# A transformer block on one core: features on partitions to the output, 512-token products, halves added and subtracted, parity checks as matrix products

## The chip, the cores and the metric

The kernel runs on one core of a Trainium2 chip. The metric is device time in microseconds (us) of one execution. The engines are TensorE (PE, with weight loads as PEld), VectorE (DVE), ScalarE (ACT), GpSimd (POOL) and SyncE (SP), which here only issues DMAs.

## The reference

8192 tokens of 256 features; everything is float32.

```python
xn = layernorm(x)                              # over the 256 features, eps 1e-5
D  = fractal_dimension(xn)                     # one number, from the first 1024 values of xn
x1 = ifft(fft(xn) * wave_filter(D)).real       # a circulant 256x256 matrix applied to each token
lat  = x1 @ W_el + b_el                        # 24 latents
bits = sigmoid(lat) > 0.5
syn  = bits @ H.T > 0.5                        # 12 checks; H is 12x24 of zeros and ones
w    = syn.sum(-1)
# if 0 < w <= 3: flip the bits among the first 12 whose check is set; else leave them
attn = x1 + corrected @ W_le + b_le
ffn  = gelu(xn @ w1 + b1) @ w2 + b2            # 256 -> 1024 -> 256, exact gelu
out  = x + attn + ffn
```

## The kernel before

The tokens are cut into 16 chunks of 512 (`CHUNKS`, 4 tiles of 128 tokens each). A float32 operand of a product is split into a part rounded to fp32r (`_hi`) and the rest (`_lo`); each product is the sum of three, hi x hi, lo x hi and hi x lo.

- **up** (L741): w1 is stationary, the normalised input `xT` (features on partitions, 2 blocks `k` of 128) is moving: for each of 8 hidden blocks `m`, 6 products of 512 columns into one of two PSUM banks `p_h`. ACT makes `h` (gelu, L378) and rounds it to `h_hi` (L386), DVE makes `h_lo` (`hidden_lo`, L508).
- **down** (L771): the hidden tile is stationary and w2 moving, so the output has tokens on partitions: for each `m` and each of the 4 tiles 3 products of 256 columns into `p_o`. It waits for the whole of `h_lo`.
- **wave_products** (L790): filter and latents together, 280 columns (256 + 24), 6 for each tile of 128 tokens, into `p_c`, a pair of tiles at a time.
- **correct** (L519, DVE): the bits of a pair of tiles, with tokens on partitions, are weighed with powers of two and summed to a word, and-ed with 12 masks, counted, compared; ten small instructions, most with a wait for the one before (`hops`). PE transposes the result (L805), ACT copies it (L388), and `le_products` (L814) adds it with W_le and both biases (256 columns a tile).
- **The input** comes in twice: rows `x_sb` (kept for all chunks, for statistics and as the residual to which DVE adds in place, L511 and L552) and columns `xt_sb`. Mean and 1/std of each token are made on DVE and POOL, written to DRAM, read back broadcast to all partitions (`rows_sb`, with the four values of a kind 32 bytes apart), and POOL subtracts (L333), DVE multiplies (L498), ACT rounds (L370), DVE takes the rest (L503).

Each engine has its own order of work, written out by hand. Chunk 0 is the prologue: DVE normalises it from rows, PE transposes it, weights are split (`w1_hi`, `w1_lo`, ...), D is found, and the filter's matrix and latent weights are made (`circulant` L868, `latent_products` L875). A loop of 14 chunks follows, each with the branch (filter, bits, correction) of the chunk before, and a last chunk with two branches. PE's order in a chunk is: up m, then pieces of the branch at some m, then down m-2 (L823). DVE's order is at L562, SP's at L294 to L309.

Of the kernel before, what the change touches and what calls it, by code (L numbers as in the profile page):

```python
# [11 lines left out]
P = 128  # L39
# [7 lines left out]
PAIRS = CT // 2  # L47
CE = E + LAT
# [11 lines left out]
HALF = CT // 2  # L60
HEAD = 1
LAST_PIECES = ((0, 2), (2, 3), (3, 4))
PRIMED = 1
ROWS_LE = LAT + 2
# [10 lines left out]
K_POW2 = K_WK + 2 * KB  # L75
K_END = K_POW2 + LAT


def build(nc, x, xt, w_el, b_el, w_le, b_le, w1, b1, w2, b2, consts, prefixes, basis, masks, out):
    ctx = ExitStack()  # L80
    with ctx:
# [20 lines left out]
        w1_f = sb("w1_f", [P, KB, HID], F32)  # L102
        w1_hi = sb("w1_hi", [P, KB, HID], F32R)
        w1_lo = sb("w1_lo", [P, KB, HID], F32R)
        w2_f = sb("w2_f", [P, MB, E], F32)
        w2_hi = sb("w2_hi", [P, MB, E], F32R)
        w2_lo = sb("w2_lo", [P, MB, E], F32R)
        b1_sb = sb("b1_sb", [P, MB], F32)
        con = sb("con", [P, K_END], F32)
        mask_sb = sb("mask_sb", [P, SYN], I32)  # L110
        bel_sb = sb("bel_sb", [P, LAT], F32)
        wel_sb = sb("wel_sb", [P, KB, LAT], F32)
        basis_sb = sb("basis_sb", [P, KB, E], F32)
# [14 lines left out]
        fr_tab = sb("fr_tab", [NS, 3, FR * E], F32)  # L128
        fr_part = sb("fr_part", [NS, FR * E], F32)
# [20 lines left out]
        le_mid = sb("le_mid", [ROWS_LE, E], BF16)  # L150
# [834 lines left out]
```

## Time and profile before

| | us |
|---|---|
| median of 3 runs (445.8 to 446.93) | 446.28 |
| the profiled execution | 446.24 |
| its span | 444.2 |
| PE busy | 433.6 (98%) |
| DVE busy | 298.0 (67%) |
| ACT busy | 197.5 (44%) |
| POOL busy | 80.0 (18%) |

The span goes from the first to the last instruction of the execution. PE's busy time is the union of overlapping matmul records, each of which holds its pipeline's drain, so the price of a product is read from the distance between two starts. A query of the trace prints the start, the duration, the engine, the line, the tiles (written, then read), the shape and how many alike were merged; in brackets the idle time before and what ended it.

### The profile page before, as it was taken

Reading aid. Unit: us, or ns where it says so; the run is one execution under the profiler, and the core shown is the slowest. Engines: PE = TensorE matmul, PEld = TensorE weight load, DVE = VectorE, ACT = ScalarE, POOL = GpSimd, SP = SyncE. Lnnn points to the kernel's source line nnn. Section 1 sums busy time; section 2 is a strip of 40 time slices with the busy share of each in tenths; the row PEclk is TensorE's granted clock in tenths of the full one; section 3 lists DMA queues with packets and bytes.
Section 4 is the critical chain, followed back from the end, with each engine's and each line's share of the span. In section 5 each row is a group of like instructions: output and inputs, shape, how many; then the busy total and the mean of one; then the engine's idle time right before and its main releaser. Section 6 shows DMA issues by size and latency. Waiting matters only on the chain.

```text
span 444.2 us, 8446 instructions
## 1 busy us (share of the span) xinstructions
PE 433.6 (98%) x2856; PEld 391.5 (88%) x2856; DVE 298.0 (67%) x722; ACT 197.5 (44%) x332; POOL 80.0 (18%) x72
## 2 busy tenths in 40 slices
PE   7969999999999999999999999999999999999996
PEld 4858899899999999898998989989999999989996
DVE  5977586665767666576765667666575767667544
ACT  4742444444354344535443444444435434443431
POOL 1640211203013130301213012130401313030000
PEclk9997999999999999999999999999999999999999
DMA  8541302223130232303213230232313022020101
GB/s 236 169 168 48 120 2 90 101 71 118 50 110 29 71 118 71 118 15 99 76 71 118 71 116 2 82 108 71 118 45 106 38 71 71 24 71 5 44 24 49
DMA packets 17789, 35.38 MB, mean 80 GB/s; under 512 B 5331, under 2 KB 7533, under 8 KB 17773
## 3 DMA queue, kind: packets, MB, share of 16 engines
q1 hardware_dynamic: 17778, 35.24, 23.9%
q8 instruction: 6, 0.10, 0.1%
q14 instruction: 5, 0.04, 0.0%
HBM read 26.76 MB, written 8.45 MB: 79 GB/s over the span
## 4 chain that ended last, share of the span: by engine, by line
PE 91%; DMA 3%; POOL 2%; DVE 1%; ACT 1%; issue 1%; SPq 0%; DVEq 0%; POOLq 0%
PE p_o L786 40%; PE p_h L766 38%; PE p_c L800 11%; PE p_c L819 2%; DMA w_f<-L_ffn_w 1%; DMA rows_sb<-rows_dram 1%; PE p_g L810 1%; POOL xt_sb L333 1%; DMA rows_dram<-mv 1%; POOL w_lo L342 1%; PE p_c L872 0%; POOL mv L324 0%; DVE xt_sb L498 0%; DVE x_sb L602 0%; ACT w_hi L419 0%
## 5 line engine op out<-in xcount | busy, mean ns | idle before, releaser
L378 ACT ACTIVATE h<-p_h,b_sb 128x512 f32<-128x512 f32 x128 | 88.1, 689 | 213.0 <-PE p_h L766 213.0
L786 PE MATMUL p_o<-w_hi,h_hi 128*128 128x256 f32 x512 | 149.7, 292 | 4.1 <-DVE h_lo L508 4.1
L786 PE MATMUL p_o<-w_lo,h_hi 128*128 128x256 f32 x512 | 145.4, 284 | 0.0
L786 PE MATMUL p_o<-w_hi,h_lo 128*128 128x256 f32 x512 | 145.2, 284 | 0.0
L508 DVE TENSOR_TENSOR h_lo<-h,h_hi 128x512 fp32r<-128x512 f32 x128 | 94.6, 740 | 52.3 <-ACT h_hi L386 50.0
L786 PEld LDWEIGHTS p_o<-w_hi,h_hi 128*128 128x128 f32 x512 | 98.1, 192 | 7.1 <-DVE h_lo L508 4.7
L786 PEld LDWEIGHTS p_o<-w_lo,h_hi 128*128 128x128 f32 x512 | 98.3, 192 | 1.9
L786 PEld LDWEIGHTS p_o<-w_hi,h_lo 128*128 128x128 f32 x512 | 98.2, 192 | 0.0
L766 PE MATMUL p_h<-xT_hi,w_hi 128*128 128x512 f32 (+1 forms) x258 | 82.1, 399 | 0.6 <-ACT xT_hi L433 0.6
L386 ACT CAST h_hi<-h 128x512 fp32r<-128x512 f32 x128 | 79.5, 621 | 5.6
L766 PE MATMUL p_h<-xT_hi,w_lo 128*128 128x512 f32 (+1 forms) x258 | 79.9, 391 | 0.0
L766 PE MATMUL p_h<-xT_lo,w_hi 128*128 128x512 f32 (+1 forms) x258 | 79.5, 389 | 0.0
L333 POOL TENSOR_TENSOR xt_sb<-xt_sb,rows_sb 128x512 f32<-128x512 f32 x30 | 53.8, 1814 | 83.9 <-DMA rows_sb<-rows_dram 83.9
L498 DVE TENSOR_TENSOR xt_sb<-xt_sb,rows_sb 128x512 f32<-128x512 f32 x30 | 54.0, 1838 | 20.5 <-POOL xt_sb L333 20.5
L766 PEld LDWEIGHTS p_h<-xT_hi,w_lo 128*128 128x128 f32 x258 | 48.3, 188 | 11.1
L766 PEld LDWEIGHTS p_h<-xT_lo,w_hi 128*128 128x128 f32 x258 | 48.3, 188 | 11.0
L321 POOL TENSOR_TENSOR var_eps<-mv,eps 128x4 f32<-128x4 f32 (+1 forms) x17 | 3.8, 225 | 228.3 <-DVE mv L483 228.3
L766 PEld LDWEIGHTS p_h<-xT_hi,w_hi 128*128 128x128 f32 x258 | 41.0, 190 | 2.1 <-ACT w_hi L419 0.8
L560 DVE TENSOR_TENSOR x_sb<-p_c,x_sb 128x512 f32 (+1 forms) x32 | 22.1, 690 | 27.3 <-PE p_c L819 27.3
L800 PE MATMUL p_c<-c_hi,xT_hi 128*128 128x280 f32 x128 | 37.4, 292 | 0.0
L800 PE MATMUL p_c<-c_lo,xT_hi 128*128 128x280 f32 x128 | 37.4, 292 | 0.0
L800 PE MATMUL p_c<-c_hi,xT_lo 128*128 128x280 f32 x128 | 36.9, 289 | 0.0
(95 smaller groups left out, 323.3 us busy)
## 6 DMA issues: line engine op xcount, KB each, us to landing
out<-x_sb SPq DMA_DIRECT2D x31, 256.0 KB, 2.3
x_sb<-L_attn_x SPq DMA_DIRECT2D x15, 512.0 KB, 5.3
xt_sb<-xt SPq DMA_DIRECT2D x15, 512.0 KB, 3.6
rows_sb<-rows_dram SPq DMA_DIRECT2D x15, 512.0 KB, 4.1
w_f<-L_ffn_w SPq DMA_DIRECT2D x3, 512.0 KB, 7.1
x_sb<-L_attn_x SPq DMA_DIRECT2D x2, 256.0 KB, 2.8
w_f<-L_ffn_w SPq DMA_DIRECT2D x2, 256.0 KB, 5.2
basis_sb<-basis SPq DMA_DIRECT2D x1, 256.0 KB, 4.9
```

Source lines behind the costliest of these rows:

```text
L333: nc.gpsimd.tensor_tensor(seg, seg, row_values(par, 0), ALU.subtract).then_inc(centred, 1)
L342: nc.gpsimd.tensor_tensor(w1_lo[:, :, cols], w1_f[:, :, cols], w1_hi[:, :, cols].bitcast(F32), ALU.subtract).then_inc(w1_ready, 1)
L378: nc.scalar.activation(h[m % 2][:], p_h[:, m % 2, :], ACT.Gelu, bias=b1_sb[:, m:m + 1]).then_inc(gelu_done, 1)
L386: nc.scalar.copy(h_hi[m % HR][:], h[m % 2][:]).then_inc(h_hi_done, 1)
L498: nc.vector.tensor_tensor(seg, seg, row_values(par, 1), ALU.mult).then_inc(scaled, 1)
L508: nc.vector.tensor_tensor(h_lo[m % HR][:], h[m % 2][:], h_hi[m % HR][:].bitcast(F32), ALU.subtract).then_inc(h_lo_done, 1)
L560: nc.vector.tensor_tensor(seg, p_c[:, :, 0:E], seg, ALU.add).then_inc(wave_added if last else pair_out, 1)
L766: last = mm(p_h[:, m % 2, tok], w[:, k, m * P:(m + 1) * P], xt[par][:, k, tok], start=(n == 0), stop=(n == 3 * KB - 1))
L786: last = mm(p_o[:, j, :], hp[r][:, tok], w[:, m, :], start=(m == 0 and n == 0 and j % 2 == 0), stop=(m == MB - 1 and n == 2), skip_group_c ...
L800: last = mm(p_c[:, r, 0:CE], xt[par][:, k, tok], cc[:, k, :], start=(n == 0), stop=False, skip_group_check=True)
L810: last = nc.tensor.transpose(p_g[0:3 * SEG, r * P:(r + 1) * P], cor[:, r, :, :].rearrange("p a s -> p (a s)"), id_bf[:])
L819: last = mm(p_c[:, r, 0:E], cor_T[:, r * P:(r + 1) * P], le3[:], start=False, stop=True, skip_group_check=True)
```

## The change

Output, too, has features on partitions from now on, and the host's arrangement of `xt` and `out` follows (moves only).

- The two halves of the features are added and subtracted: `uv` holds x0+x1 and x0-x1 (POOL, `turn`), and w1, w2, the latent weights and W_le are added and subtracted in the same way and halved, once in the prologue (POOL and DVE add, ACT halves and rounds). The filter matrix has the blocks [[A, B], [B, A]], so in this basis it is two 128x128 blocks, A+B and A-B. At the end DVE adds sum and difference to the two halves of the input columns with the bias, four operations of 128x512 in place of the additions before (`add_differences`, `add_sums`).
- **down** has w2 stationary and the hidden block moving: for each `m` 6 products of 512 columns, and it waits for `h_hi` first, for `h_lo` before the last two. The filter adds into the same banks (`p_o`, now two pairs of banks, one for each parity of the chunk).
- **latents**: 6 products of 512 columns for a chunk; the 24 latents stand three times on 96 rows. The bits come out with latents on partitions: `take_bits` is one DVE operation on 96x512, `count` a product with H, `take_checks` a comparison, `weigh` a product with ones, `correct` two operations, `le_products` two products of 512 columns. The word, the masks, the transposes and ACT's copy go.
- The columns `xt_sb` of all chunks stay in SBUF (the last four chunks' places first hold the weights' sums and differences); the rows `x_sb` have two buffers and serve the statistics alone. `rows_sb` is contiguous for each kind of value, and holds twice the mean.
- PE's prologue runs four up blocks ahead of down (`LOOK`). Chunk 1 runs its branch two blocks later than the others (`at`). In the last chunk the two branches, `last_down` with one signal for each half, and four stores.

```diff
-PAIRS = CT // 2
-CE = E + LAT
+HF = E // 2
...
+        xt_sb = sb("xt_sb", [P, CHUNKS, KB, CTOK], F32)
+        x_sb = [sb(f"x_sb{i}", [P, CT, E], F32) for i in range(2)]
+        rows_sb = [sb(f"rows_sb{i}", [P, 2, CTOK], F32) for i in range(2)]
+        uv = sb("uv", [P, KB, CTOK], F32)
...
+        p_o = ps("p_o", [P, 2, 2, BANK], F32)
+        p_l = ps("p_l", [P, BANK], F32)
+        p_g = ps("p_g", [P, BANK], F32)
...
+            def load_x(c):
+                par = c % 2
+                if c >= 2:
+                    sp.wait_ge(stat_done, c)
...
+            def turn_w1(n):
+                cols = slice(W1_PARTS[n][0] * P, W1_PARTS[n][1] * P)
+                pool.wait_ge(w1_in[n], 16)
+                for k, op in ((0, ALU.add), (1, ALU.subtract)):
+                    nc.gpsimd.tensor_tensor(w1_t[:, k, cols], w1_f[:, 0, cols], w1_f[:, 1, cols],
+                                            op).then_inc(w1_turned[n], 1)
...
+            def turn(c, par, first=False):
+                pool.wait_ge(xt_in[par], all_to(c, par))
+                if first:
+                    pool.wait_ge(t_done, 2)
+                else:
+                    pool.wait_ge(t_lo, KB * c)
+                halves = xt_sb[:, bass.ds(c, 1), :, :].rearrange("p c k t -> p (c k) t")
+                nc.gpsimd.tensor_tensor(uv[:, 0, :], halves[:, 0, :], halves[:, 1, :], ALU.add).then_inc(turned, 1)
+                nc.gpsimd.tensor_tensor(uv[:, 1, :], halves[:, 0, :], halves[:, 1, :], ALU.subtract).then_inc(turned, 1)
...
+            def take_bits(c):
+                dve.wait_ge(lat_done, c + 1)
+                nc.vector.tensor_scalar(bits[:], p_l[0:ROWS, :], -1.0, bel_sb[:, 0:1],
+                                        ALU.mult, ALU.is_lt).then_inc(bits_done, 1)
+            def take_checks(c):
+                dve.wait_ge(counted, c + 1)
+                nc.vector.tensor_scalar(syn[:], p_g[0:ROWS, :], 0.5, None, ALU.is_gt).then_inc(syn_done, 1)
+            def correct(c):
+                dve.wait_ge(weighed, c + 1)
+                nc.vector.scalar_tensor_tensor(out=flips[:], in0=p_g[0:ROWS, :], scalar=3.0, in1=syn[:],
+                                               op0=ALU.is_le, op1=ALU.mult).then_inc(flips_done, 1)
+                dve.wait_ge(flips_done, c + 1)
+                nc.vector.tensor_tensor(cor[:], bits[:], flips[:], ALU.not_equal).then_inc(cor_done, 1)
...
+            def add_differences(c, par, tok=slice(0, CTOK), added=diff_added):
+                xc = columns(c, tok)
+                nc.vector.scalar_tensor_tensor(out=xc[:, 0, :], in0=p_o[:, par, 1, tok], scalar=bias[:, 0:1],
+                                               in1=xc[:, 0, :], op0=ALU.add, op1=ALU.add).then_inc(added, 1)
+                nc.vector.scalar_tensor_tensor(out=xc[:, 1, :], in0=p_o[:, par, 1, tok], scalar=-1.0,
+                                               in1=xc[:, 1, :], op0=ALU.mult, op1=ALU.add).then_inc(added, 1)
+            def add_sums(c, par, tok=slice(0, CTOK), done=summed):
+                xc = columns(c, tok)
+                nc.vector.tensor_tensor(xc[:, 0, :], p_o[:, par, 0, tok], xc[:, 0, :], ALU.add).then_inc(done, 1)
+                nc.vector.scalar_tensor_tensor(out=xc[:, 1, :], in0=p_o[:, par, 0, tok], scalar=bias[:, 1:2],
+                                               in1=xc[:, 1, :], op0=ALU.add, op1=ALU.add).then_inc(done, 1)
...
             def chunk(c, par):
+                b = c - 1
+                statistics(c + 1, 1 - par)
+                dve.wait_ge(stats_made, c + HEAD + 2)
                 hidden_lo(c, 0)
-                hops(statistics(c + 1, 1 - par))
+                aggregate(1 - par)
+                take_bits(b)
                 hidden_lo(c, 1)
-                aggregate(1 - par)
-                correct(c - 1, 0, hops)
+                take_checks(b)
                 hidden_lo(c, 2)
+                correct(b)
                 hidden_lo(c, 3)
-                add_wave(c - 1, 0)
+                centre(c + 1, 1 - par)
+                scale(c + 1, 1 - par)
                 hidden_lo(c, 4)
-                scale(c + 1, 1 - par)
+                dve.wait_ge(le_done, c)
+                add_differences(b, 1 - par)
                 hidden_lo(c, 5)
-                correct(c - 1, 1, hops)
+                dve.wait_ge(diff_added, KB * c)
+                add_sums(b, 1 - par)
+                turned_lo(c + 1, 1 - par, 0)
                 hidden_lo(c, 6)
-                transposed_lo(c + 1, 1 - par, 0)
-                transposed_lo(c + 1, 1 - par, 1)
+                turned_lo(c + 1, 1 - par, 1)
                 hidden_lo(c, 7)
-                add_wave(c - 1, 1)
...
+            def last_chunk(c, par):
+                b = c - 1
+                hidden_lo(c, 0)
+                take_bits(b)
+                hidden_lo(c, 1)
+                take_checks(b)
+                hidden_lo(c, 2)
+                correct(b)
+                hidden_lo(c, 3)
+                hidden_lo(c, 4)
+                dve.wait_ge(le_done, c)
+                add_differences(b, 1 - par)
+                hidden_lo(c, 5)
+                take_bits(c)
+                dve.wait_ge(diff_added, KB * c)
+                add_sums(b, 1 - par)
+                hidden_lo(c, 6)
+                take_checks(c)
+                hidden_lo(c, 7)
+                correct(c)
+                dve.wait_ge(tail_down, 1)
...
+            def down(c, par, m, first=False):
+                pe.wait_ge(h_hi_done, MB * c + m + 1)
+                if m == 0 and not (isinstance(c, int) and c < 2):
+                    pe.wait_ge(summed, KB * (c - 1))
                 for n, (m0, _) in enumerate(W2_PARTS):
                     if first and m == m0:
                         pe.wait_ge(w2_ready, n + 1)
                 r = m % HR
...
+                for a in range(2):
+                    for w in (w2_hi, w2_lo):
+                        mm(p_o[:, par, a, :], w[:, m, a, :], h_hi[r][:], start=(m == 0 and w is w2_hi), stop=False,
+                           skip_group_check=True)
+                pe.wait_ge(h_lo_done, MB * c + m + 1)
+                for a in range(2):
+                    last = mm(p_o[:, par, a, :], w2_hi[:, m, a, :], h_lo[r][:], start=False, stop=False,
+                              skip_group_check=True)
+                last.then_inc(down_done, 1)
+            def last_down(c, par, m):
+                pe.wait_ge(h_lo_done, MB * c + m + 1)
+                r = m % HR
+                for a in (1, 0):
+                    for n, (w, hp) in enumerate(((w2_hi, h_hi), (w2_lo, h_hi), (w2_hi, h_lo))):
+                        last = mm(p_o[:, par, a, :], w[:, m, a, :], hp[r][:], start=False, stop=(n == 2),
+                                  skip_group_check=True)
+                    last.then_inc(tail_down, 1)
...
+            def latents(c, par, first=False):
+                if not first:
+                    pe.wait_ge(bits_done, c)
+                n = 0
+                for k in range(2):
+                    for w, xp in ((cw_hi, xT_hi), (cw_lo, xT_hi), (cw_hi, xT_lo)):
+                        last = mm(p_l[0:ROWS, :], w[:, k, :, :].rearrange("p g l -> p (g l)"), xp[par][:, k, :],
+                                  start=(n == 0), stop=(n == 5))
+                        n += 1
+                last.then_inc(lat_done, 1)
...
+            def filtered(c, par):
+                for k in range(2):
+                    for w, xp in ((c_hi, xT_hi), (c_lo, xT_hi), (c_hi, xT_lo)):
+                        last = mm(p_o[:, par, k, :], w[:, k, :], xp[par][:, k, :], start=False, stop=False,
+                                  skip_group_check=True)
...
+            def count(c, first=False):
+                pe.wait_ge(bits_done, c + 1)
+                if not first:
+                    pe.wait_ge(flips_done, c)
+                mm(p_g[0:ROWS, :], code[0:LAT, 0:ROWS], bits[0:LAT, :], start=True, stop=True).then_inc(counted, 1)
+            def weigh(c):
+                pe.wait_ge(syn_done, c + 1)
+                mm(p_g[0:ROWS, :], code[0:SYN, ROWS:2 * ROWS], syn[0:SYN, :], start=True, stop=True).then_inc(weighed, 1)
+            def le_products(c, par):
+                pe.wait_ge(cor_done, c + 1)
+                for a in range(2):
+                    last = mm(p_o[:, par, a, :], le3[:, a, :], cor[:], start=False, stop=False, skip_group_check=True)
...
+                at = (2, 3, 4, 5, 6) if first_branch else (0, 1, 2, 3, 5)
                 for m in range(MB):
                     up(c, par, m)
...
+                    if m == at[0]:
+                        if first_branch:
+                            pe.wait_ge(c_ready, 1)
...
+                    if m == 7:
+                        filtered(c, par)
+                        count(c)
+                down(c, par, MB - 2)
+                weigh(c)
+                le_products(c, par)
+                last_down(c, par, MB - 1)
...
+            for m in range(LOOK):
+                up(0, 0, m, first=True)
             for m in range(MB):
...
+                down(0, 0, m, first=True)
+                if m + LOOK < MB:
+                    up(0, 0, m + LOOK, first=True)
+                if m == 3:
+                    pe.wait_ge(logged, 1)
+                    mm(p_g[:, 0:1], con[0:NS, K_COEF:K_COEF + P], fr_ln[:], start=True, stop=True).then_inc(dim_made, 1)
                 if m == 6:
...
+                    circulant()
+            latent_weights()
```

## Rows read from the trace of the kernel before

**Rows 1.** The page, section 2: the granted clock in 40 slices.

```profile
PEclk9997999999999999999999999999999999999999
```

**Rows 2.** Windows: stretch, its length, busy PE, PEld, DVE, ACT, POOL, clock, DMA.

```profile
221.09:247.50 26.41, 26.41 (x177) 24.05 (x177) 17.67 (x44) 11.93 (x21) 4.76 (x4) 1.00 0.23 80
410.37:444.20 33.83, 30.35 (x210) 27.64 (x208) 16.66 (x53) 11.29 (x20) 0.00 (x0) 1.00 0.11 40
```

**Rows 3.** PE's timeline: first products of blocks, start and duration.

```profile
40.57 0.71 PE L766 MATMUL p_h<-xT_hi,w_hi 128*128 128x512 f32 x2
...
228.27 0.29 PE L800 MATMUL p_c<-c_hi,xT_hi 128*128 128x280 f32 x1
...
229.82 0.62 PE L766 MATMUL p_h<-xT_hi,w_hi 128*128 128x512 f32 x2
...
231.18 0.28 PE L786 MATMUL p_o<-w_hi,h_hi 128*128 128x256 f32 x1
...
232.61 0.63 PE L766 MATMUL p_h<-xT_hi,w_hi 128*128 128x512 f32 x2
...
234.00 0.28 PE L786 MATMUL p_o<-w_hi,h_hi 128*128 128x256 f32 x1
...
235.43 0.27 PE L810 MATMUL p_g<-id_bf,cor 128*96 128x128 bf16 x2
...
236.99 0.40 PE L819 MATMUL p_c<-le,cor_T 96*128 96x256 bf16 x2
...
238.66 0.64 PE L766 MATMUL p_h<-xT_hi,w_hi 128*128 128x512 f32 x2
...
410.37 0.63 PE L766 MATMUL p_h<-xT_hi,w_hi 128*128 128x512 f32 x2
```

**Rows 4.** Groups by line and shape: busy, mean ns, idle before.

```profile
L508 DVE TENSOR_TENSOR h_lo<-h,h_hi 128x512 fp32r<-128x512 f32 x128 | 94.6, 740 | 52.3 <-ACT h_hi L386 50.0 <-DVE wave L681 0.4
L378 ACT ACTIVATE h<-p_h,b_sb 128x512 f32<-128x512 f32 x128 | 88.1, 689 | 213.0 <-PE p_h L766 213.0
L386 ACT CAST h_hi<-h 128x512 fp32r<-128x512 f32 x128 | 79.5, 621 | 5.6
L498 DVE TENSOR_TENSOR xt_sb<-xt_sb,rows_sb 128x512 f32<-128x512 f32 x30 | 54.0, 1838 | 20.5 <-POOL xt_sb L333 20.5
L333 POOL TENSOR_TENSOR xt_sb<-xt_sb,rows_sb 128x512 f32<-128x512 f32 x30 | 53.8, 1814 | 83.9 <-DMA rows_sb<-rows_dram 83.9
L517 DVE TENSOR_TENSOR x_sb<-p_o,x_sb 128x512 f32 x28 | 18.0, 685 | 11.1 <-PE p_o L786 11.1
L342 POOL TENSOR_TENSOR w_lo<-w_f,w_hi 128x1024 fp32r<-128x1024 f32 x1 | 2.4, 2411 | 6.5 <-ACT w_hi L419 6.5
```

**Rows 5.** Timelines of SP and POOL in one chunk: row numbers out and their use.

```profile
233.13 0.33 SPq L263 DMA_DIRECT2D rows_dram<-mv  x1
238.81 3.56 POOL L333 TENSOR_TENSOR xt_sb<-xt_sb,rows_sb 128x512 f32<-128x512 f32 x2 [5.70 <-DMA rows_sb<-rows_dram]
```

**Rows 6.** The prologue: windows (as Rows 2), then timelines of PE and DVE.

```profile
30.00:35.00 5.00, 1.34 (x6) 1.34 (x7) 4.16 (x23) 0.62 (x1) 0.00 (x0) 0.68 0.01 2
35.00:40.00 5.00, 5.00 (x27) 4.64 (x27) 2.93 (x10) 0.81 (x3) 0.00 (x0) 0.64 0.00 0
33.66 0.58 PE L786 MATMUL p_o<-w_hi,h_hi 128*128 128x256 f32 x1 [4.07 <-DVE h_lo L508]
29.92 0.16 DVE L659 TENSOR_SCALAR fr_d<-p_c 128x1 f32<-128x1 f32 x1
35.10 0.73 DVE L690 TENSOR_SCALAR basis_w<-basis_sb,wave 128x256 f32<-128x256 f32 x2
```

**Rows 7.** Timelines of POOL and DVE: a subtraction of each at the same time.

```profile
17.48 2.83 POOL L349 TENSOR_TENSOR w_lo<-w_f,w_hi 128x1024 fp32r<-128x1024 f32 x1
18.33 2.54 DVE L508 TENSOR_TENSOR h_lo<-h,h_hi 128x512 fp32r<-128x512 f32 x1
```

**Rows 8.** The end: PE's last product and DVE's last additions.

```profile
440.44 0.28 PE L786 MATMUL p_o<-w_hi,h_lo 128*128 128x256 f32 x1
441.13 0.75 DVE L602 TENSOR_TENSOR x_sb<-p_o,x_sb 128x256 f32<-128x256 f32 x2
```

More of the change, by code:

```diff
@@ L290, in _ @@
-            sp.dma_start(le_f[LAT + 1:LAT + 2, :], b2[None, :]).then_inc(le_in, 16)
+            sp.dma_start(wel_sb[:, :, :], w_el.rearrange("(k p) l -> p k l", p=P)).then_inc(wel_in, 16)
+            sp.dma_start(code_f[:], codes).then_inc(code_in, 16)
+            sp.wait_ge(pool_set, 3)
+            for n in range(GROUPS):
+                sp.dma_start(bel_sb[n * SEG:n * SEG + LAT, :], b_el[:, None]).then_inc(bel_in, 16)
+            sp.dma_start(le_f[:], w_le).then_inc(le_in, 16)
+            with nc.allow_non_contiguous_dma(reason="1 KB once"):
+                for n, b in enumerate((b_le, b2)):
+                    sp.dma_start(bias2[:, n, :], b.rearrange("(k p) -> p k", p=P)).then_inc(bias_in, 16)
@@ new lines, in _ @@
+            nc.vector.tensor_tensor(wel_t[:, 1, :], wel_sb[:, 0, :], wel_sb[:, 1, :], ALU.subtract).then_inc(wel_turned, 1)
+            for n in range(KB):
+                turned_lo(1, 1, n)
+            dve.wait_ge(c_made, 1)
+            nc.vector.tensor_copy(c_f[:, :, :].rearrange("p a e -> p (a e)"), p_l[:, 0:E]).then_inc(c_copied, 1)
+            dve.wait_ge(bias_in, 32)
+            then(nc.vector.tensor_tensor(bias[:], bias2[:, 0, :], bias2[:, 1, :], ALU.add))
+            dve.wait_ge(cw_made, 1)
@@ new lines, in _ @@
+            dve.wait_ge(le_in, 16)
+            rows = le3[0:LAT, :, :]
+            nc.vector.tensor_tensor(le_t[:, 0, :], le_f[:, 0:HF], le_f[:, HF:E], ALU.add)
+            then(nc.vector.tensor_tensor(le_t[:, 1, :], le_f[:, 0:HF], le_f[:, HF:E], ALU.subtract))
+            then(nc.vector.tensor_scalar(rows, le_t[:], 0.5, None, ALU.mult))
+            then(nc.vector.scalar_tensor_tensor(out=le_r1[:], in0=le_t[:], scalar=0.5, in1=rows,
+                                                op0=ALU.mult, op1=ALU.subtract))
@@ L716, in _ @@
-            base = links[0]
-            per_chunk = 1 + 7 * PAIRS
-            def hopper(start):
-                n = [0]
-                def hop(ins):
-                    n[0] += 1
-                    ins.then_inc(link, 1)
-                    dve.wait_ge(link, start + n[0])
-                return hop
-            with dve.Fori(0, (CHUNKS - 2) // 2) as i:
+            dve.wait_ge(bel_in, 16 * GROUPS)
+            dve.wait_ge(xt_in[0], 16)
+            chunk(1, 1)
+            with dve.Fori(1, CHUNKS // 2 - 1) as i:
```

699 lines of the change are left out of this document (308 added, 391 removed).

## The prediction

> **What bounds the kernel now.** I read the page first: TensorE (PE) is busy 98% of the span at a granted clock that is full except early on [rows 1]. A window over one steady chunk then shows that it is busy for all of its 26.41 us, while DVE has 17.67, ACT 11.93 and POOL 4.76 [rows 2]. So in the body only PE's own work counts, and the first start of an up product in chunk 1 (40.57) and in chunk 15 (410.37) lie 14 x 26.41 apart [rows 2, 3]. Three pieces remain: the prologue, 40.57 us; 14 periods, 369.8; the last chunk, 33.83. They make the span, 444.2; the execution took 446.24, so 2.04 lie around it, and the median of the runs, 446.28, is the same. A change under 0.3%, about what a measurement of this kernel can tell, counts as none.
>
> PE's durations overlap (the drain is in them), so I price by starts. Six 512-column up products take 1.36 us behind wave products (229.82 to 231.18), 227 ns each, and 1.39 behind down products. Twelve 256-column down products take 1.43, 119 ns each; twelve of 280 columns 1.55, 129 ns; two transposes and an up 1.56, so 0.17 for the two; two `le` products and a down block 1.67, so 0.24 for the two [rows 3]. A straight line through 256 and 512 columns is 11 ns for each product plus 0.422 ns a column.
>
> **The body.** The halves leave PE's columns where they were. Before, a chunk has 48 x 512 (up), 96 x 256 (down), 24 x 280 (wave and latents), 4 x 256 (`le`): 56,896 columns, and 4 transposes. The circulant splits into two 128x128 blocks, which halves the filter to 6 x 512, but the 24 latent columns become 6 products that stream 512 columns for 96 rows of output; two bit products and two `le` products of 512 join: 48+48+6+6+1+1+2 = 112 products, 57,344 columns. What falls is their number, 176 to 112. At 227.5 ns a product the new period is 25.5 us, 0.9 shorter. The fixed part explains 64 x 11 ns = 0.7; the rest are the 0.03 that up loses behind each down block. Bound above: if that step stays, each six-product block costs 1.385, and the period is 112 x 0.2308 = 25.85; below, 25.4. I take 25.5, since the step appears only behind 256-column products. Latent weights of 96 columns and the bfloat16 bit products have no row of this width; the `le` rows, 120 ns for 256 columns in bfloat16, lie with the others.
>
> The Trainium skill, "TensorE: Matmul & The Clock Gate", section "Back-to-back issue gap", gives N/2.4 + 2.5 ns between isolated products, 2.6 ns for each pair merged instead of the rows' 11; by it both periods would be about 24.2 us and nearly equal. The rows of this trace are slower at both widths.
>
> **What hides the other engines.** DVE's chunk becomes: 8 hidden_lo, 3 centre and scale, 2 turned_lo and 4 output additions, near 0.69 each, four bit operations over 96x512 from PSUM (0.69 above, half that for the all-bfloat16 one), and statistics as before: 16 us of 25.5. The 16 small hopped steps go. Centre and scale cost 1.8 each before, with strided row values on DVE and POOL [rows 4]; contiguous rows put them near hidden_lo's 0.69 (bounds 0.69 and 1.84, 3.5 us more a chunk, still under the period). ACT loses two copies of `cor`. I then laid the new order against PE. Latents go out at 1.4 us of a chunk, take_bits ends at 4.6, count at 7.05; take_checks ends at 7.8, weigh is at 9.8; flips and cor are ready at 11.3, `le` is at 15.5. Waiting DVE instructions queue hidden_lo behind them: take_checks holds hidden_lo(2) for 0.9 us, the wait for `le_done` holds hidden_lo(5) until 17.4, and down 5 needs it near 22. None reaches PE. The row numbers leave on SP and reach POOL 5.7 us after issue [rows 5], here 11.4 to 12.4 us into the chunk; DVE's centre stands in front of hidden_lo(4), which down 4 needs at 19.5: covered by 4 us. p_o's second pair of banks takes the wait for additions away, which PE did not feel anyway. The input columns are kept for all chunks, so SP's load of x waits only for statistics, and its store for `summed`: a chunk early, no cost. The tightest place is hidden_lo(7): h_hi is ready at 22.8 (up 7 ends 21.4, then 0.69 and 0.62 on ACT [rows 4]), and the second part of down 7 needs h_lo at 25.0.
>
> **The prologue.** Now it holds a stall: PE stands 4.07 us until h_lo at 33.66, behind DVE's filter chain, and the granted clock averages 0.68 and 0.64 in the two stretches from 30 to 40, so it stood at 1.2 GHz for part of each and at 2.4 for the rest [rows 6]. The change puts four up blocks ahead of down, so the stall's place goes, but adds links. Two additions of 0.42 for each half of the normalised rows: both transposes 0.9 to 1.5 later. Weights are added and subtracted first (0.6 to 1.8 a POOL operation by the rows for 512 elements [rows 4]) before ACT can halve and round them. DVE operations with two SBUF inputs queue behind those: the h_lo of 18.33 took 2.54 us instead of 0.69 beside a POOL subtraction that ran until 20.31 [rows 7]. Worked through in order: up 0 at 9.3, up 2 at 15.5 (w1 part 1), down 0 at 19.3 (w2_lo(0) behind hidden_lo(1)), up 4 at 21.5 (w1_lo(2)), up 7 until 31.1, then the dimension product. DVE's chain from there to the weighed basis took 29.92 to 35.83 with h_lo and xT_lo inside [rows 6]; less the xT_lo it is 5.3: circulant at 36.7, down 7 held by centre, scale and hidden_lo(7) until 39.4, turned_lo and the copy of `c_f` to 41.5, latent weights to 42.4. Chunk 1 starts there, 1.8 later than now (bounds: 40.5, if the lock costs nothing and the order closes up; 46, if the clock falls again in the idle places from 35.5 on and each link has its upper price).
>
> Chunk 1 runs the branch two blocks later. take_checks waits for count behind up 4 (54.9) and holds hidden_lo(2); correct waits for weigh behind up 5 and holds hidden_lo(3). Down 2, down 3 and down 6 wait 0.5, 1.2 and 0.3: 2.0 us once (0.5 to 3).
>
> **The end.** The last chunk has two branches: 16 more products, 128 x 0.2275 = 29.1 us, drain 0.16. Behind weigh PE waits: 0.4 drain, flips 0.69, cor 0.35 to 0.69, 0.3 of hops, less the 0.23 of weigh itself: 1.7. Now only 0.41 lie between the last product (ends 440.72) and DVE, whose 0.75 and the store end the span 3.48 after it [rows 8]. After, the two 512-column difference additions start at tail_down 1, 0.7 before the end of the products, four 256-column additions of 0.37 follow, then the same store: 4.9. Together 35.9 against 33.83, 2.1 more (1 to 3.5).
>
> **Sum.** 42.4 + (25.5 + 2.0) + 13 x 25.5 + 35.9 = 437.3 of span; with 2.04, 439.3 us, 1.6% less. In differences: body -12.8, prologue +1.8, chunk 1 +2.0, end +2.1.
>
> **The rivals.** (a) The step stays, period 25.85: +4.9, 444.2; for it speaks that up behind down costs it now, against it that nothing of 256 columns is left. (b) Fewer products save nothing: columns alone set the period, 26.4, and what the rows show as a price of each product is paid some other way. Then the three additions remain, 446.2 + 5.9 = 452.1. The straight line of the rows is against it. The Trainium skill's rule on the issue gap, cited above, points to this case. (c) On the other side: POOL's turn of the next chunk starts when turned_lo(1) ends, 21.7, and its two operations lie exactly before hidden_lo(7). A DVE subtraction waited for a POOL one to end [rows 7]; with 1.8 each [rows 4] hidden_lo(7) ends at 26.0 instead of 25.0 and PE waits 1 us a chunk: +14, 453. At 1.2 each, a half of the 1024-element subtraction, it ends at 24.8 and costs nothing; slower than before from a stall of 0.5 a chunk on. The Trainium skill, "SBUF — State Buffer", section "Who interferes with whom", says that DVE with two SBUF inputs contends with a POOL instruction that reads SBUF, and that the loser blocks for its whole length; [rows 7] agree, 2.54 against 0.69. That rule changes (c)'s chance, not the sum. (d) The prologue ends at 46 or chunk 1 waits more, clock low again: 442 to 447. (e) The four up blocks ahead make the prologue as short as 40.5: 437 or less.
>
> **How the numbers follow.** Forecast 0.55, (a) 0.12, (b) 0.03, (c) 0.08, (d) 0.12, (e) 0.10. Likeliest time 439.3. Its own range is 436 to 442.5; 434 to 447 takes in (a), (d) and (e) and leaves (b) and (c) out. Faster 0.83 (forecast, a, e, most of d), same 0.06 (rest of d), slower 0.11 (b, c).
>
> **What would show it.** A steady window with PE full and 25.5 us, products of 512 columns 227 ns apart in down blocks too: the body. 26.4 and PE full: (b). PE idle before down's h_lo product, released by DVE: (c). The granted clock by 5 us from 30 to 45, and the first up of chunk 1: the prologue. Waits of PE behind h_lo in chunk 1, and one behind `cor` at the end. It is wrong if an engine other than PE sets the period, or if prologue and end together lose more than 12.8.

## The result and the profile after

The changed kernel takes 450.76 us (median of 4 runs, 450.48 to 451.68), the kernel before 446.04 beside it (445.32 to 446.93). The ratio is 1.0108, with a 95% interval of 1.0085 to 1.0132. It is slower by about 1%, a small but clear difference, where 1.6% faster was forecast. The profiled execution took 450.8 with a span of 449.0; the sum of the prediction had 437.3 for the span, so 11.7 us have to be found.

The page of the changed kernel, sections 1 and 2 and some groups of section 5 (busy, mean ns, idle before):

```profile
span 449.0 us, 5615 instructions
PE 430.9 (96%) x1828; PEld 329.7 (73%) x1828; DVE 266.0 (59%) x524; ACT 190.7 (42%) x298; POOL 82.5 (18%) x96
...
PEclk9999999999999999999999999999999999999998
...
L494 DVE TENSOR_TENSOR h_lo<-h,h_hi 128x512 fp32r<-128x512 f32 x128 | 88.7, 693 | 106.3 <-ACT h_hi L396 106.2
```

PE is still the busy engine, at 96%, and its granted clock is full in nearly every slice; the fall of [rows 1] in the fourth slice is gone. A slice of 11 us hides a shorter one: a window over 10 to 15 us of this run has a clock of 0.72, where the kernel before had 1.00. DVE fell from 298.0 to 266.0 us, and hidden_lo from 740 to 693 ns [rows 4]: the engines off the path got shorter, as forecast. Windows over chunk 1, a steady chunk and the last chunk, columns as in [rows 2]:

```profile
44.10:72.34 28.24, 27.14 (x115) 20.17 (x114) 19.64 (x45) 11.89 (x19) 5.48 (x6) 1.00 0.21 64
229.18:255.32 26.14, 26.14 (x114) 20.31 (x112) 15.00 (x29) 11.52 (x18) 4.37 (x5) 1.00 0.25 80
412.16:449.00 36.84, 30.62 (x129) 22.49 (x127) 15.66 (x26) 10.47 (x16) 0.00 (x0) 0.96 0.08 28
```

| stretch | forecast | measured | miss |
|---|---|---|---|
| prologue, to the first up of chunk 1 | 42.4 | 44.10 | +1.7 |
| chunk 1 | 27.5 | 28.24 | +0.7 |
| 13 steady chunks | 331.5 | 339.8 | +8.3 |
| last chunk and end | 35.9 | 36.84 | +0.9 |

The body shrank by 0.27 us a chunk instead of 0.9, and it was PE's own time that did not go: PE is busy for all 26.14 us. PE's timeline in that chunk, as in [rows 3]:

```profile
229.18 0.62 PE L771 MATMUL p_h<-xT_hi,w_hi 128*128 128x512 f32 x2
...
230.54 0.40 PE L815 MATMUL p_l<-xT_hi,cw_hi 128*96 128x512 f32 x1
...
231.93 0.62 PE L771 MATMUL p_h<-xT_hi,w_hi 128*128 128x512 f32 x2
...
233.30 0.39 PE L824 MATMUL p_o<-xT_hi,c_hi 128*128 128x512 f32 x1
...
234.68 0.62 PE L771 MATMUL p_h<-xT_hi,w_hi 128*128 128x512 f32 x2
...
235.58 0.61 PE L771 MATMUL p_h<-xT_hi,w_lo 128*128 128x512 f32 x2
236.13 0.41 PE L832 MATMUL p_g<-spare,code 24*96 24x512 bf16 x1
236.47 0.50 PE L789 MATMUL p_o<-h_hi,w_hi 128*128 128x512 f32 x1
236.81 0.39 PE L789 MATMUL p_o<-h_hi,w_lo 128*128 128x512 f32 x1
...
237.96 0.61 PE L771 MATMUL p_h<-xT_hi,w_hi 128*128 128x512 f32 x2
```

Priced by starts, the latents cost 231.93 - 230.54 = 1.39 and the filter 234.68 - 233.30 = 1.38. A block of six up products is 1.36, and a down block without a small product the same (242.61 to 243.97). All this is as forecast, 227 to 232 ns a product. From 234.68 to 237.96 lie an up block, count and a down block: 3.28 us, less 2 x 1.36 leaves 0.56 for a product that was put at 0.23. Weigh, three microseconds on, comes to 0.57. The three distances around count are 0.32 (the second product of the merged 235.58 row starts 0.23 after the first), 0.34 and 0.34, each about 0.1 above 0.227. Two such products a chunk, 0.32 to 0.34 us too dear each, account for the 0.64 by which the period missed.

Two explanations were left for the body. Theory R (rows): the small products are dear because they stand on 24 and 12 rows of the array, between products of 128 rows. Its rival, S: they cost what they cost because a bfloat16 product or another bank of PSUM stands between fp32r ones, whatever the rows. The pair of `le` products, also bfloat16, stands on 96 rows and cost 0.24 for two before and 0.47 after, which speaks for R but doesn't show it. For the prologue, theory T: the additions and subtractions of the weights cost it; the rival is the new order of its work.

### The profile page after: what moved, and what is told of

Same layout as the page of the kernel before. It is cut to its first block, busy times and chain, and to the rows that moved or that the text cites. A ratio compares the mean times of both kernels' runs of the same rounds, so it can differ in the third digit from the quotient of the medians.

```text
span 449.0 us, 5615 instructions
## 1 busy us (share of the span) xinstructions
PE 430.9 (96%) x1828; PEld 329.7 (73%) x1828; DVE 266.0 (59%) x524; ACT 190.7 (42%) x298; POOL 82.5 (18%) x96
## 4 chain that ended last, share of the span: by engine, by line
PE 87%; DVE 9%; ACT 2%; issue 1%; DMA 1%; POOL 0%; DVEq 0%; POOLq 0%
PE p_h L771 36%; PE p_o L789 25%; PE p_o L794 12%; PE p_o L824 5%; PE p_l L815 5%; PE p_o L842 2%; DVE h_lo L494 1%; PE p_g L836 1%; PE p_g L832 1%; DMA x_sb<-L_attn_x 1%; ACT h L388 1%; DVE fr_part L651 1%; DVE fr_part L657 0%; DVE uv L612 0%; DVE xt_sb L586 0%
## 5 line engine op out<-in xcount | busy, mean ns | idle before, releaser
L789 PE MATMUL p_o<-h_hi,w_hi 128*128 128x512 f32 x254 | 105.9, 417 | 1.0 <-DVE w_lo L599 1.0
L789 PE MATMUL p_o<-h_hi,w_lo 128*128 128x512 f32 x254 | 99.1, 390 | 0.0
L794 PE MATMUL p_o<-h_lo,w_hi 128*128 128x512 f32 x254 | 79.0, 392 | 1.4 <-DVE h_lo L494 1.3
L350 POOL TENSOR_TENSOR uv<-xt_sb 128x512 f32 (+1 forms) x15 | 20.6, 1371 | 231.6 <-DVE xT_lo L489 231.6
L789 PEld LDWEIGHTS p_o<-h_hi,w_hi 128*128 128x128 f32 x254 | 47.7, 188 | 18.5 <-issue 8.4
L794 PEld LDWEIGHTS p_o<-h_lo,w_hi 128*128 128x128 f32 x254 | 47.4, 188 | 13.1 <-DVE h_lo L494 3.2
L789 PEld LDWEIGHTS p_o<-h_hi,w_lo 128*128 128x128 f32 x254 | 47.8, 188 | 8.6
L351 POOL TENSOR_TENSOR uv<-xt_sb 128x512 f32 (+1 forms) x15 | 26.6, 1774 | 0.0
L519 DVE SCALAR_TENSOR_TENSOR xt_sb<-p_o,bias,xt_sb 128x512 f32 (+1 forms) x16 | 12.0, 751 | 18.7 <-PE p_o L842 17.3
L465 DVE BATCH_NORM_STATS2 stats<-x_sb 128x6 f32<-128x256 f32 x60 | 21.0, 412 | 0.0
L380 ACT CAST xT_hi<-uv 128x512 fp32r<-128x512 f32 x30 | 18.5, 617 | 4.7 <-DVE uv L483 4.7
```

What stands on the lines that cost most here:

```text
L350: nc.gpsimd.tensor_tensor(uv[:, 0, :], halves[:, 0, :], halves[:, 1, :], ALU.add).then_inc(turned, 1)
L351: nc.gpsimd.tensor_tensor(uv[:, 1, :], halves[:, 0, :], halves[:, 1, :], ALU.subtract).then_inc(turned, 1)
L380: nc.scalar.copy(xT_hi[par][:, k, :], uv[:, k, :]).then_inc(t_hi, 1)
L465: last = nc.vector.bn_stats(stats[:, j, :], x_sb[par][:, j, :])
L789: mm(p_o[:, par, a, :], w[:, m, a, :], h_hi[r][:], start=(m == 0 and w is w2_hi), stop=False, skip_group_check=True)
L794: last = mm(p_o[:, par, a, :], w2_hi[:, m, a, :], h_lo[r][:], start=False, stop=False, skip_group_check=True)
```

## The experiments

The experiments on the body and on the prologue make one kind of edit each. The second is built on the changed kernel, all others on the first, so their "kernel without the edit" is e1_rows96. All but the first and the last are one execution each, so they are read from the windows and starts of their traces rather than from the total time.

**Rows of count and weigh.** The code tile is padded with zeros to 96 rows; the bit tiles have 96 rows anyway.

```diff
-code = sb("code", [LAT, 2 * ROWS], BF16)
+code = sb("code", [ROWS, 2 * ROWS], BF16)      # set to 0 once, on POOL
-mm(p_g[0:ROWS, :], code[0:LAT, 0:ROWS], bits[0:LAT, :], ...)
+mm(p_g[0:ROWS, :], code[0:96, 0:ROWS], bits[0:96, :], ...)
-mm(p_g[0:ROWS, :], code[0:SYN, ROWS:2 * ROWS], syn[0:SYN, :], ...)
+mm(p_g[0:ROWS, :], code[0:96, ROWS:2 * ROWS], syn[0:96, :], ...)
```

> The two bit products of a chunk (count with 24 rows of weights, weigh with 12) take 0.57 us each from the block before to the block behind, where 0.23 was forecast; here both stand on 96 rows (zeros added to the weights, the moving rows are there already), nothing else. Theory R, the price is that of the few rows: each falls to 0.23, the steady period from 26.14 to 25.46, the time from 450.8 to 450.8 - 16 x 0.68 = 439.9 us (438.5 to 441.5). Rival S, the price is that of a lone bfloat16 product between fp32r ones and its wait, whatever its rows: the period stays 26.14 and the time 450.8.

Measured: 441.63 us (441.01 to 442.22, 4 runs) beside 446.74 of before, ratio 0.9884 (0.9863 to 0.9906). Windows over a steady chunk and the last one, then PE's timeline around count and the weight loads there (the brackets hold idle time):

```profile
379.19:404.68 25.49, 25.49 (x114) 20.48 (x113) 13.77 (x25) 11.53 (x18) 1.32 (x3) 1.00 0.13 42
404.68:440.40 35.72, 29.51 (x129) 22.77 (x127) 15.74 (x26) 10.48 (x16) 0.00 (x0) 1.00 0.08 29
```

```profile
233.04 0.38 PE L834 MATMUL p_g<-spare,code 96*96 96x512 bf16 x1
233.07 0.58 PE L791 MATMUL p_o<-h_hi,w_hi 128*128 128x512 f32 x1
233.49 0.40 PE L791 MATMUL p_o<-h_hi,w_lo 128*128 128x512 f32 x1
```

```profile
232.81 0.12 PEld L834 LDWEIGHTS p_g<-spare,code 96*96 96x96 bf16 x1
233.04 0.19 PEld L791 LDWEIGHTS p_o<-h_hi,w_hi 128*128 128x128 f32 x1
```

The loads of the changed kernel at the same place:

```profile
236.13 0.11 PEld L832 LDWEIGHTS p_g<-spare,code 24*96 24x96 bf16 x1 [0.35 <-issue]
236.47 0.19 PEld L789 LDWEIGHTS p_o<-h_hi,w_hi 128*128 128x128 f32 x1 [0.23 <-issue]
```

The period is 25.49, where 25.46 was expected, and from count to the second product of the next block it is 0.45 instead of 0.68. (The product right behind count is recorded only 0.03 after it, 233.07, so the distance is read to the second.) The same product, type, columns and bank: only the rows differ, so R stands and its rival falls. The loads show the form of it. On 96 rows the weights go in 0.23 before their product, beside the product ahead; on 24 rows the load starts with its product, and the next load, of 128 rows, waits likewise.

The median is 1.7 above the centre of what was expected and 0.1 above its range; the profiled execution, 442.22, is 2.3 above the centre. Half of these 2.3 is the clock in this execution; windows of e1_rows96:

```profile
40.00:45.00 5.00, 3.65 (x16) 2.46 (x15) 4.96 (x11) 1.62 (x3) 1.63 (x2) 0.92 0.41 148
45.00:50.00 5.00, 5.00 (x18) 3.96 (x17) 4.40 (x14) 2.98 (x5) 0.88 (x1) 0.74 0.00 0
```

PE had stood for 1.35 of the 5 us before 45, and the granted clock averaged 0.92 and then 0.74, so it was at 1.2 GHz for part of each stretch. Chunk 1 took 29.18 here, and 28.03 in a later kernel with the same chunk 1 (p4_tail) at a full clock: 1.15. Most of the rest is an expectation set too high. The steady period fell by 0.65 instead of 0.68, 0.4 us over 13; in chunk 1, where PE waits for h_lo, only 0.21 of the 0.68 shows (28.24 against 28.03), as its two marked waits grow from 0.26 and 0.72 to 0.45 and 0.90; and in the last chunk 1.12 instead of 1.36 shows (36.84 against 35.72), as the last weigh has its price inside PE's wait for `cor`.

**How many rows are enough.** Count on 32 rows, weigh on 64, otherwise the same edit.

> count on 32 rows and weigh on 64, zeros added. Theory R with the price tied to the smallest group of 32 rows: count still costs 0.57, weigh 0.23, period 25.80, time about 445.4. R with the price tied to anything under 96: both 0.57, period 26.14, 450.8. R with the price tied to rows that are no multiple of 32: both 0.23, period 25.46, 439.9. Rival S: both 0.57.

Measured: 450.85 us, span 449.0, the changed kernel's again. PE's timeline:

```profile
236.18 0.41 PE L834 MATMUL p_g<-spare,code 32*96 32x512 bf16 x1
236.52 0.50 PE L791 MATMUL p_o<-h_hi,w_hi 128*128 128x512 f32 x1
236.85 0.39 PE L791 MATMUL p_o<-h_hi,w_lo 128*128 128x512 f32 x1
...
239.46 0.41 PE L838 MATMUL p_g<-spare,code 64*96 64x512 bf16 x1
239.81 0.50 PE L791 MATMUL p_o<-h_hi,w_hi 128*128 128x512 f32 x1
240.14 0.40 PE L791 MATMUL p_o<-h_hi,w_lo 128*128 128x512 f32 x1
```

Both distances behind both products are 0.33 to 0.35. So 64 rows pay the whole price, 96 none. It is not graded by the rows, and the padding by itself (the memset, the larger tile) is not what helped.

**Is it paid for each product, or for the change of shape?** The `le` pair on 32 rows.

```diff
-mm(p_o[:, par, a, :], le3[:, a, :], cor[:], ...)
+mm(p_o[:, par, a, :], le3[0:SEG, a, :], cor[0:SEG, :], ...)
```

> As the kernel with both bit products on 96 rows, but the two products that add W_le use the first 32 of their 96 rows; the two finer parts of W_le are left out of the computation. The reverse test: theory R says that the pair, which costs 0.47 us now, pays the price once (0.81, period 25.80) if it belongs to the change of shape between neighbours, or twice (1.15, period 26.14) if to each product of few rows. Rival S: the pair stays at 0.47, period as with 96 rows.

Measured: 447.0 us. Windows and PE's timeline:

```profile
382.00:407.81 25.81, 25.81 (x114) 20.40 (x112) 14.41 (x27) 11.53 (x18) 1.79 (x4) 1.00 0.13 41
...
243.85 0.60 PE L844 MATMUL p_o<-spare,le 32*128 32x512 bf16 x2
244.39 0.50 PE L791 MATMUL p_o<-h_hi,w_hi 128*128 128x512 f32 x1
244.72 0.40 PE L791 MATMUL p_o<-h_hi,w_lo 128*128 128x512 f32 x1
```

The period grows by 25.81 - 25.49 = 0.32, once the 0.34 and not twice, although there are two products. The price is that of going to few rows and back. The loads say the same: in this trace the first of the pair's loads starts with its product, 243.85.

**The price of a product.** The line through 256 and 512 columns (11 ns a product) was read from different instructions of one trace. Here the down products of e1_rows96 are cut in two again, in the same places, with the same operands.

```diff
+for t in (slice(0, GTOK), slice(GTOK, CTOK)):
-    mm(p_o[:, par, a, :], w[:, m, a, :], h_hi[r][:], ...)
+    mm(p_o[:, par, a, t], w[:, m, a, :], h_hi[r][:, t], ...)
```

> As the kernel with both bit products on 96 rows, but each of the 48 down products of a chunk is cut in two of 256 columns (96, as many as before the change). My line for the price of a product (11 ns each plus 0.422 ns a column, and 0.03 us where an up block follows a down block of 256 columns) gives 0.53 + 0.2 = 0.7 us more a chunk: period 26.2, time about 451. The rival that columns alone set the period: no change against the kernel with 96 rows, 25.46 and 439.9.

Measured: 451.53 us, and the period is the distance of these two starts, 26.23:

```profile
362.33 0.40 PE L819 MATMUL p_l<-xT_hi,cw_hi 128*96 128x512 f32 x1
...
388.56 0.40 PE L819 MATMUL p_l<-xT_hi,cw_hi 128*96 128x512 f32 x1
```

That is 0.74 a chunk more than 25.49, for 48 more products and the same columns. 48 x 11 ns is 0.53, and eight up blocks behind 256-column products at 0.03 (one takes 1.39 here, 375.36 to 376.75, against 1.36) are 0.24, together 0.77. The saving that the change was priced on is real.

**The weights' work.** w1 and w2 are read as they are loaded, without sums and differences on POOL.

```diff
-turn_w1(0); turn_w2(0); turn_w1(2); turn_w2(1)     # and turn_w1(1) on DVE
-nc.scalar.mul(w1_hi[:, :, cols], w1_t[:, :, cols], 0.5)
+nc.scalar.mul(w1_hi[:, :, cols], w1_f[:, :, cols], 0.5)
```

> On the kernel with 96 rows. The sums and differences of w1 and w2 are left out of the computation: ACT and DVE split the weights as they came; all else stays. In the profile after, chunk 1 starts at 44.1 us, 3.5 later than before the change (40.57) and 1.7 later than forecast. Theory T, the prologue is late through the added weights' work on POOL and DVE and the DVE operations that wait for it: up 2 waits 1.4 less, down 0 and up 4 start 1.5 to 2.5 earlier, the comparison operations on DVE fall from 2.3 to 1.2 us where POOL is free, and chunk 1 starts at 40.5 to 42. Rival U, PE's own order decides (the dimension product stands behind up 7, and DVE's filter chain behind it): chunk 1 starts less than 1 us earlier, 43 or later.

Measured: 436.6 us. PE's wait for the second part of w1 in the prologue of p1_noturn, then two of its waits in e1_rows96:

```profile
19.71 0.74 PE L769 MATMUL p_h<-xT_hi,w_hi 128*128 128x512 f32 x2 [0.80 <-DVE w_lo L591]
```

```profile
22.76 0.74 PE L773 MATMUL p_h<-xT_hi,w_hi 128*128 128x512 f32 x2 [0.82 <-DVE w_lo L594]
33.88 0.38 PE L939 MATMUL p_g<-fr_ln,con 5*128 5x1 f32 x2 [1.26 <-DVE fr_part L659]
```

Chunk 1 starts at 39.57 against 44.00, so the weights' work costs 4.4 us: 3.05 of it are there at up 4, the rest comes up to the dimension product, whose 1.26 wait is gone. Theory T stands and rival U falls; the gain is larger than T said (chunk 1 at 40.5 to 42, down 0 and up 4 by 1.5 to 2.5). The clock isn't the reason: from 10 to 15 us it was 0.66 in e1_rows96 and 1.00 here, but there up 2, which comes next, waited 1.06 us for `w_lo`, and it starts at 16.18 in b1_best, where that clock was 0.50, against 15.99. One of the three 5x1024 comparison operations stays long (2.31), beside POOL's turn of chunk 1, which has moved up. The new order without the weights' work is 1.0 shorter than before's 40.57, with a full clock where before had 0.68 and 0.64 from 30 to 40 [rows 6].

**One lock taken out.** The stretch ahead of the dimension product, changed kernel, DVE and POOL:

```profile
29.68 2.02 DVE L599 SCALAR_TENSOR_TENSOR w_lo<-xt_sb,w_hi 128x1024 fp32r<-128x1024 f32 x1
31.62 2.30 DVE L657 SCALAR_TENSOR_TENSOR fr_part<-spare,fr_cnt 5x1024 bf16<-5x1024 f32 x1
...
28.34 2.27 POOL L350 TENSOR_TENSOR uv<-xt_sb 128x512 f32<-128x512 f32 x1
30.58 2.27 POOL L351 TENSOR_TENSOR uv<-xt_sb 128x512 f32<-128x512 f32 x1
```

In p2_turnlate POOL's two operations on chunk 1's columns wait until the logarithm, which follows these, is done.

```diff
+pool.wait_ge(logged, 1)
 turn(1, 1, first=True)
```

> On the kernel with 96 rows. POOL's turn of chunk 1 (28.3 to 32.9 us in the profile after) waits until DVE has the logarithm ready, so that the three 5x1024 operations and the split of the second w2 part, 2.3, 2.0 and 2.3 us there, don't run beside it. If a DVE operation with two SBUF inputs waits for POOL's instruction to end: the last two fall to 1.2 to 1.3, the dimension product comes 1 to 1.8 us earlier (33.98 there), chunk 1 starts 0.5 to 1.5 earlier. Rival: the durations stay, since 5 lanes by 1024 elements are slow by themselves beside any work: no change.

Measured: 441.62 us, no gain. DVE's timeline of p2_turnlate:

```profile
8.87 2.78 DVE L615 TENSOR_TENSOR uv<-rows_sb 128x256 f32<-128x256 f32 x2
...
30.43 1.22 DVE L602 SCALAR_TENSOR_TENSOR w_lo<-xt_sb,w_hi 128x1024 fp32r<-128x1024 f32 x1
31.57 1.27 DVE L660 SCALAR_TENSOR_TENSOR fr_part<-spare,fr_cnt 5x1024 bf16<-5x1024 f32 x1
...
34.65 1.23 DVE L674 TENSOR_SCALAR wave<-con,fr_d 128x2 f32<-128x2 f32 x1
```

The two operations take 1.22 and 1.27 instead of 2.02 and 2.30 (1.23 and 1.27 in p1_noturn, where POOL is idle beside them too), so the lock is confirmed. The Trainium skill, "SBUF — State Buffer", section "Who interferes with whom", says that a DVE instruction with two SBUF inputs contends with a POOL instruction that reads SBUF, and that the port they share is an exclusive lock. The traces agree: in the changed kernel the two end 1.1 us behind the end of the POOL operation beside them (31.70 and 33.92, POOL 30.61 and 32.85), about the time that they take alone. But the lock was moved, not removed. An operation of the filter chain on two elements of each partition took 1.23 instead of 0.29 beside the same POOL work, and in this execution the second half of x's sums lost 2 us at 8.87 to POOL's first w2 operation, which it beats otherwise (0.76 in e1_rows96). Chunk 1 started at 44.54, so the expected 0.5 to 1.5 did not come: a miss. The late start is part of it. Counted from up 4 (23.61 against 22.76), the dimension product comes 1.4 sooner than in e1_rows96 (33.37 against 33.88), as expected, and chunk 1 only 0.3: the gain is lost between the two.

**Chunk 1.** The branch steps of chunk 1 go out one or two blocks sooner (the steps are latents, filter, count, weigh, `le`, each with the up block that it follows).

```diff
-at = (2, 3, 4, 5, 6) if first_branch else (0, 1, 2, 3, 5)
+at = (2, 3, 3, 4, 5) if first_branch else (0, 1, 2, 3, 5)
```

> On the kernel with 96 rows. In chunk 1 count, weigh and the W_le products go one up block earlier (behind up 3, 4, 5, not 4, 5, 6). In the profile after DVE stood 5.1 us in front of count's result with hidden_lo(2) queued behind, and 2.5 us in front of weigh's with hidden_lo(3) behind; PE lost 2.1 us in chunk 1. If that queue is the cause: PE's waits for h_lo in chunk 1 (0.45 and 0.90 in the kernel with 96 rows) go and chunk 1 is 1 to 2 us shorter. If the late split of the filter weights is the cause, PE waits elsewhere as long.

Measured: 439.27 us. The changed kernel's two marked waits of PE in chunk 1, then the window over chunk 1 in p3_order1:

```profile
58.84 0.73 PE L794 MATMUL p_o<-h_lo,w_hi 128*128 128x512 f32 x2 [0.26 <-DVE h_lo L494]
63.13 0.73 PE L794 MATMUL p_o<-h_lo,w_hi 128*128 128x512 f32 x2 [0.72 <-DVE h_lo L494]
```

```profile
44.14:70.21 26.07, 25.93 (x115) 20.50 (x115) 20.55 (x45) 11.88 (x19) 7.00 (x7) 1.00 0.27 82
```

26.07 against 28.03 in p4_tail, which keeps the old order: 1.96 us, and no product waits for h_lo. It was DVE's queue, with take_checks and correct ahead of hidden_lo, as the prediction had it.

**The end.** Count goes ahead of the filter in the last chunk, and weigh ahead of down 6.

```diff
-filtered(c, par); count(c)
+count(c); filtered(c, par)
-down(c, par, MB - 2); weigh(c)
+weigh(c); down(c, par, MB - 2)
```

> On the kernel with 96 rows. In the last chunk count goes ahead of the filter products and weigh ahead of down 6, so that the filter and down 6 lie between weigh and the W_le products, which stood 1.24 us on DVE's correction. That wait goes: the last chunk is 1.0 to 1.3 us shorter. Rival: DVE reaches the correction no earlier, since hidden_lo(7) stands ahead of it, and the wait moves to weigh or down 7: under 0.4.

Measured: 439.75 us. The wait of the changed kernel, and the last chunk of p4_tail (e1_rows96: 35.72, above):

```profile
442.03 0.60 PE L842 MATMUL p_o<-spare,le 96*128 96x512 bf16 x2 [1.24 <-DVE spare L511]
```

```profile
403.53:437.90 34.37, 29.41 (x129) 22.77 (x127) 15.74 (x26) 10.48 (x16) 0.00 (x0) 0.97 0.08 31
```

1.35 shorter, a little more than the 1.0 to 1.3 expected: the wait of 1.24 is covered by the filter and down 6, and the rival falls.

**All together.** e1_rows96 with the orders of p3_order1 and p4_tail, and POOL's first w2 operation held until the sums of x are made (`pool.wait_ge(uv0_done, 2)` ahead of `turn_w2(0)`).

> The parts together: both bit products on 96 rows, the branch of chunk 1 one up block earlier, the last chunk with count ahead of the filter and weigh ahead of down 6, and POOL's addition of the first w2 part waits until DVE has added the second half of the normalised rows (in one execution it came first, and that DVE operation waited 2 us for it). If the pieces add: prologue 44.0, chunk 1 26.1, 13 periods of 25.5, last chunk 34.5 = 436.1 of span, 437.9 us, a ratio near 0.981 to the kernel before. Rival: the pieces overlap or the clock falls in chunk 1 (it fell in one execution, 44 to 48 us): 439 to 441.

Measured: 438.36 us (438.27 to 439.38, 5 runs) beside 445.73 (444.96 to 446.8, 9 runs), ratio 0.9842 (0.9825 to 0.986): 1.6% faster than the kernel before, and about 12 us faster than the changed one. Its chunk 1 took 26.07 and its last chunk 34.39, as the pieces say. Its clock was 0.50 from 10 to 15 us and 0.66 from 35 to 40, and chunk 1 starts at 44.34, so the prologue gained nothing from the added wait.

## Why the prediction was wrong

**The step that failed** is the one sentence that let two products in unpriced: "Latent weights of 96 columns and the bfloat16 bit products have no row of this width; the `le` rows, 120 ns for 256 columns in bfloat16, lie with the others." The `le` rows are of 96 rows, the bit products of 24 and 12. The nearest rows agreed in type and differed in the one size that mattered, and no upper bound was put beside them. Measured, each costs 0.57 us against 0.23. That is 0.64 us in each of the 13 steady periods, 8.3 of the 11.7 us; 0.2 more shows in chunk 1 and 1.1 in the last chunk, which has four of them. With the rows mended the kernel took 441.63, inside the range of 434 to 447 and 2.3 above the likeliest time; the prologue's miss, 44.00 for 42.4, is 1.6 of it. As changed it took 450.76, outside, near the times of (b) and (c) but by the mechanism of neither.

**The body's mechanism was right.** 512-column products are 227 ns apart in all blocks, the step of 0.03 behind down is gone (rival (a) falls: 25.49), and cutting them again costs 0.74 (e4_down256). Rival (b), columns alone, looked right from the total, with a period of 26.14 close to its 26.4, but for another reason: e4_down256 and e1_rows96 have the same columns and 0.74 between them. (By columns alone the period would be 26.6, as they rise from 56,896 to 57,344; the prediction wrote 26.4.) The Trainium skill's isolated gap of N/2.4 + 2.5 ns ("TensorE: Matmul & The Clock Gate", "Back-to-back issue gap") would have given an estimate of 48 x 2.5 ns = 0.12 there; the traces show 0.74.

**Rival (c) fell, narrowly.** In the changed kernel, POOL and DVE in the steady chunk:

```profile
251.60 1.29 POOL L350 TENSOR_TENSOR uv<-xt_sb 128x512 f32 x1 [16.96 <-DVE xT_lo L489]
252.84 1.81 POOL L351 TENSOR_TENSOR uv<-xt_sb 128x512 f32 x1
...
252.82 0.69 DVE L494 TENSOR_TENSOR h_lo<-h,h_hi 128x512 fp32r<-128x512 f32 x1 [1.43 <-ACT h_hi L396]
```

POOL's first operation took 1.29, not the 1.8 of the strided ones in [rows 4], and ended as h_hi came. hidden_lo(7) went in at 252.82, 0.02 ahead of the second, and PE used it at 254.86. PE is busy for all 339.82 us of the 13 steady chunks, so (c) cost nothing in any of them. It was close: had POOL's second gone first, at 1.29 us like the first, and hidden_lo(7) ended 1.1 behind it as in p2_turnlate's comparison above, that would be 255.2 and PE would stand 0.4 us a chunk (an estimate). That the order came out the other way is luck; the prediction had (c) at 0.08.

**The prologue** was mis-sized: +3.5 us, not +1.8. By the prediction's own steps (changed kernel against forecast): up 2 16.09 (15.5), down 0 20.43 (19.3), up 4 22.87 (21.5), the dimension product 33.98 (31.1), circulant 39.50 (36.7), chunk 1 44.10 (42.4). 1.4 was lost at the weights by up 4; 1.3 more is the wait for the dimension product behind the locked DVE operations, which the sum did not have (it named the lock, and let the product follow up 7 at once); 1.1 came back at the end, where chunk 1 starts 4.6 behind the circulant instead of 5.7. The clock was full from 30 to 45 in that execution, so (d)'s fall was not part of it; falls after 35 show in e1_rows96 and b1_best.

**Chunk 1 and the end were right in the main.** Chunk 1 lost 2.1 to its period (2.0), at down 2 and down 3 about as forecast, but down 6 did not wait and down 0 did (h_lo at 50.92, 0.3 late), so the closeness of the sum is in part luck; with 96 rows chunk 1 lost 2.5 (28.03 against 25.49). The end had a wait of 1.24 (1.7) and 4.98 from the end of the last product (444.02) to the end of the span (4.9). What the end missed is the small products, 1.1, less the 0.5 by which the wait was put too high. The other engines' cover held: centre and scale went from 1.8 to 0.68.

**The sizes of the edits** on e1_rows96 also add up: its span of 440.4, less 1.15 of the clock, 1.96 of chunk 1 and 1.35 of the end, is 435.9; b1_best has 436.3, and its prologue is 0.34 longer.

## What to carry to other kernels

Price a small product between full ones by the rows it stands on, too, and not by its columns or type alone. Here it was enough to pad its contraction with zeros to 96 rows, which cost nothing that the traces show. When an operation is priced by its nearest rows, list every size in which it differs from them; a size that differs and has no row wants an upper bound of its own. And where a wait on a shared port is moved, look at what stands in the new place before counting the gain.

## What the runs showed of the hardware

- A bfloat16 product of 512 columns on 12, 24, 32 or 64 rows among fp32r products on 128 rows costs 0.56 to 0.57 us where 0.23 was forecast (changed kernel, e2_rows32_64); on 96 rows it costs 0.24 (e1_rows96). A pair on 32 rows pays the difference of 0.32 once (e3_le32). In the traces the weights of the few rows are loaded with their product instead of 0.23 ahead of it, and so are those of the next full product. Where between 64 and 96 rows the border lies, and why, was not tried.
- fp32r products with a weight load each are 227 ns apart at 512 columns, in both kernels, and 119 to 120 at 256 (kernel before, e4_down256), at full clock.
- A DVE operation on 128x2 elements took 1.23 us instead of 0.29 beside POOL's reads of SBUF (p2_turnlate): small operations wait too. That it is the port is argued from the like waits of the large ones, not shown alone.
- PE's granted clock fell at different places of nearly the same prologue. From 10 to 15 us, behind 5 us in which PE was busy for 2.1 and 1.8, it averaged 0.72 in the changed kernel and 0.50 in b1_best. It fell again to 0.74 from 45 to 50 in e1_rows96, behind 3.65 busy of 5, where p4_tail, with 3.67, kept 1.00, and to 0.66 from 35 to 40 in b1_best. What made it fall in one execution and not in the other is open. The fall in e1_rows96 cost 1.15 us in chunk 1.
